# All 1024 base columns through seven block products of 512 columns, instead of 96 plain ones beside products of 464

## The reference, cut to what matters

```python
y = einsum('si,oi->so', x[b], cond_weight[id[b]])        # stage one: adapter of this element
base = einsum('td,od->to', y, base_W) + base_b            # stage two: 1024 x 1024 base product
logits = einsum('td,nd->tn', y, router_W) + router_b      # 15 router columns
probs = softmax(logits); top-8 of 15, summed per expert   # 8 gates per token
h = einsum('td,erd->ter', y, A)                           # 8 experts of rank 16 = 128 columns
out[b] = x[b] + base + einsum('ter,eor->to', h * gate, B) * 2
```

## Time and profile before

| | |
|---|---|
| median of three runs | 402.02 us |
| the profiled execution, device time | 402.37 us |
| its span, first to last instruction | 400.5 us |
| TensorE matmuls busy | 394.4 us (98%), 2102 |
| VectorE busy | 301.1 us (75%), 553 |
| ScalarE busy | 158.5 us (40%), 225 |
| granted TensorE clock, mean | 1.000 of 2.4 GHz |
| one element, in the steady part | 48.10 us |

### The profile page before, as it was taken

The page is one execution under the profiler, slowest core; times in us unless marked ns, Lnnn a source line. Parts: engine busy times, 40 slices in busy tenths (PEclk is TensorE's granted clock), DMA queues, the critical chain, the costliest instruction groups (busy, mean ns, idle before and its releaser), DMA issues.

```text
span 400.5 us, 5982 instructions
## 1 busy us (share of the span) xinstructions
PE 394.4 (98%) x2102; PEld 348.0 (87%) x2102; DVE 301.1 (75%) x553; ACT 158.5 (40%) x225; POOL 8.1 (2%) x22
## 2 busy tenths in 40 slices
PE   7999999999999999999999999999999999999996
PEld 7788888888888988889888888888888888888985
DVE  2867998799868884789658886489856799467763
ACT  4656443573146401554026620355304542144300
POOL 0002220000000000000000000000000000000000
PEclk9999999999999999999999999999999999999999
DMA  7999498830467306663076510775026830464002
GB/s 286 401 391 395 88 200 270 308 110 0 157 210 263 105 0 209 187 232 105 0 255 220 195 63 14 261 276 182 0 86 228 304 115 0 149 219 158 2 0 105
DMA packets 27133, 67.56 MB, mean 169 GB/s; under 512 B 3442, under 2 KB 14194, under 8 KB 26994
## 3 DMA queue, kind: packets, MB, share of 16 engines
q1 hardware_dynamic: 25106, 62.47, 44.2%
q0 software_dynamic: 1872, 3.90, 4.9%
q10 hardware_dynamic: 144, 1.05, 0.7%
HBM read 58.08 MB, written 8.39 MB: 166 GB/s over the span
## 4 chain that ended last, share of the span: by engine, by line
PE 97%; DMA 1%; issue 0%; SPq 0%; DVE 0%
PE y_ps L807 29%; PE y_ps L809 15%; PE pl_ps L832 7%; PE x_ps L843 6%; PE x_ps L842 6%; PE x_ps L844 6%; PE s_ps L843 6%; PE s_ps L844 6%; PE s_ps L842 6%; PE pl_ps L833 4%; PE s_ps L857 1%; PE s_ps L859 1%; PE s_ps L858 1%; DMA w_raw<-in_wT 1%; PE y_ps L820 1%; PE x_ps L859 0%
## 5 line engine op out<-in xcount | busy, mean ns | idle before, releaser
L807 PE MATMUL y_ps<-x_split,w_hi 128*128 128x512 f32 x504 | 176.0, 393 | 0.9 <-issue 0.9
L809 PE MATMUL y_ps<-x_split,w_lo 128*128 128x256 f32 x504 | 141.2, 280 | 0.0
L807 PEld LDWEIGHTS y_ps<-x_split,w_hi 128*128 128x128 f32 x504 | 94.4, 187 | 22.7 <-issue 1.4
L809 PEld LDWEIGHTS y_ps<-x_split,w_lo 128*128 128x128 f32 x504 | 95.2, 189 | 0.3
L389 ACT CAST w_hi<-w_raw 128x1024 fp32r<-128x1024 f32 x59 | 61.8, 1050 | 75.5 <-DMA w_raw<-in_wT 75.5
L511 DVE TENSOR_TENSOR w_lo<-w_raw,w_hi 128x1024 fp32r<-128x1024 f32 x59 | 72.1, 1224 | 16.8 <-ACT w_hi L389 15.1
L381 ACT COPY y_sum<-y_ps 128x256 f32<-128x256 f32 x63 | 23.4, 372 | 62.2 <-PE y_ps L809 62.1
L832 PE MATMUL pl_ps<-pl_split,y_hi 128*128 128x480 f32 x128 | 42.7, 383 | 0.0
L529 DVE TENSOR_TENSOR y_sum<-y_ps,y_sum 128x256 f32<-128x256 f32 x63 | 26.5, 420 | 19.4 <-ACT y_sum L381 19.4
L833 PE MATMUL pl_ps<-pl_split,y_lo 128*128 128x240 f32 x128 | 34.9, 273 | 0.0
L842 PE MATMUL s_ps<-st_hi,y_hi 128*128 128x464 f32 x80 | 30.4, 380 | 0.0
(11 more groups left out here) (112 smaller groups left out, 537.8 us busy)
## 6 DMA issues: line engine op xcount, KB each, us to landing
w_raw<-in_wT SPq DMA_DIRECT2D x60, 512.0 KB, 3.4
res<-in_x SPq DMA_DIRECT2D x16, 512.0 KB, 4.5
x_raw<-in_xT SPq DMA_DIRECT2D x14, 512.0 KB, 4.8
out<-res SPq DMA_DIRECT2D x13, 512.0 KB, 3.0
early_raw<-in_wT SPq DMA_DIRECT2D x4, 512.0 KB, 8.6
hi_raw<-in_base_t SPq DMA_DIRECT2D x2, 928.0 KB, 10.3
st_raw<-in_base_t SPq DMA_DIRECT2D x2, 928.0 KB, 11.9
st_raw<-in_base_t POOLq DMA_DIRECT2D x2, 928.0 KB, 9.7
```

Source lines behind the costliest of these rows:

```text
L807: nc.tensor.matmul(y_ps[:, c % 2, :], w_hi[:, s, k, :], x_split[:, k, :, :].rearrange("p s t -> p (s t)"), start=(k == 0), stop=False)
L809: mm = nc.tensor.matmul(y_ps[:, c % 2, 0:T], w_lo[:, s, k, :], x_split[:, k, 0, :], start=False, stop=(k == KC - 1))
```

## The change

The 96 plain base columns are gone. `pl_split` holds only the 144 adapter and router columns, so the first matmuls of stage two are 288 and 144 columns wide instead of 480 and 240. The blocks of the base matrix are 512 columns wide instead of 464, and so is each matmul of the block products, each DMA that loads or adds a block, and each cast and subtraction on a block. The two loads of plain columns, their two casts and two subtractions in element 0, and the two additions of plain columns into `res` in each element go. What TensorE waits for before the first matmuls of an element's stage two is now the sum `ar_sum` of the element before, not the second of these additions.

The wider blocks need room in SBUF: the transposed gate operand and two arrays used with it now lie in the second half of weight slot 3 of `w_hi`, and three small arrays share space. The number and order of TensorE's instructions are the same.

```diff
-    NP = 96
-    NH = (D - NP) // 2
-    PL = AR + NP
     DH = D // 2
-    N1, PLAIN, N2 = slice(0, NH), slice(NH, NH + NP), slice(NH + NP, D)
...
-        pl_split = sb("pl_split", [P, KC, 2, PL], F32R)
+        pl_split = sb("pl_split", [P, KC, 2, AR], F32R)
...
-        st_raw, st_hi, st_lo = split_pair("st", [P, KH, 7, NH])
+        st_raw, st_hi, st_lo = split_pair("st", [P, KH, 7, DH])
...
-        at_hwt = spot[0]
-        hwt_hi = sb("hwt_hi", [P, NT, P], F32R)
-        hwt_lo = sb("hwt_lo", [P, NT, P], F32R)
+        at_hwt = at_w + (W_SLOTS - 1) * 4 * KC * P + 4 * KH * P
+        hwt_hi = sb("hwt_hi", [P, NT, P], F32R, over=at_hwt)
+        hwt_lo = sb("hwt_lo", [P, NT, P], F32R, over=at_hwt + 4 * NT * P)
...
-            for h in range(2):
-                load_plain(h)
-            load_block(hi_raw[:, :, T4, :], 0, N1, r00_in)
+            load_block(hi_raw[:, :, T4, :], 0, H1, r00_in)
...
-                if c in (5, 6):
-                    plain_hi(c - 5)
...
-                add_plain(b)
-                dve.wait_ge(pl_added, b + 1)
...
-                        nc.tensor.matmul(pl_ps[:, t, 0:2 * PL], hi, pl_split[:, k, :, :].rearrange("p s n -> p (s n)"), start=(k == 0), stop=False)
-                        mm = nc.tensor.matmul(pl_ps[:, t, 0:PL], lo, pl_split[:, k, 0, :], start=False, stop=(k == KC - 1))
+                        nc.tensor.matmul(pl_ps[:, t, 0:2 * AR], hi, pl_split[:, k, :, :].rearrange("p s n -> p (s n)"), start=(k == 0), stop=False)
+                        mm = nc.tensor.matmul(pl_ps[:, t, 0:AR], lo, pl_split[:, k, 0, :], start=False, stop=(k == KC - 1))
...
-                dst = ps[:, at]
+                dst = ps[:, :]
...
-                pe.wait_ge(pl_added, b)
+                pe.wait_ge(ar_sum_done, b)
                 plain(b)
...
-            add_block(st_raw[:, :, T2, :], base_t[:, KH:KC, N2], t2_in)
+            add_block(st_raw[:, :, T2, :], base_t[:, KH:KC, H2], t2_in)
```

More of the change, by code:

```diff
@@ L140, in adaln_ffn_kernel @@
         shift = sb("shift", [P, NT, NR])
-        picked = sb("picked", [P, NT, NR], over=at_shift)
         row_max = sb("row_max", [P, NT])
-        prob = sb("prob", [P, NT, NR])
+        prob = sb("prob", [P, NT, NR], over=at_shift)
+        picked = sb("picked", [P, NT, NR], over=at_maps)
         row_sum = sb("row_sum", [P, NT])
@@ L149, in adaln_ffn_kernel @@
         gate_n = sb("gate_n", [P, NT, E])
+        at_ar = spot[0]
         ar_sum = sb("ar_sum", [P, NT, AR])
+        router_raw = sb("router_raw", [P, KC, NR], over=at_ar)
         def bank(name, shape):
@@ L168, in adaln_ffn_kernel @@
         ar_in = sem("ar_in")
-        pl_in = [sem(f"pl_in{h}") for h in range(2)]
         r00_in = sem("r00_in")
@@ L404, in ar_part @@
                 act.wait_ge(ar_done, 2 * b + 2)
-                nc.scalar.copy(ar_sum[:, :, :], pl_ps[:, :, PL:PL + AR]).then_inc(ar_part_done, 1)
+                nc.scalar.copy(ar_sum[:, :, :], pl_ps[:, :, AR:AR + AR]).then_inc(ar_part_done, 1)
             def make_x_hi(b):
@@ L647, in stage2 @@
                 dve.wait_ge(x_ps_done, x_adds(b, 2))
-                take(0, N2, x_ps[:, AT1]).then_inc(x_added, 1)
+                take(0, H2, x_ps[:, :]).then_inc(x_added, 1)
                 make_hwt_lo(b)
@@ L656, in stage2 @@
                 dve.wait_ge(z_added, z_adds(b, 1))
-                take(1, N2, x_ps[:, AT1]).then_inc(x_added, 1)
+                take(1, H2, x_ps[:, :]).then_inc(x_added, 1)
                 if second:
@@ L764, in _ @@
             dve.wait_ge(p1_done, 1)
-            take(0, N2, w_ps[:, AT1]).then_inc(p1_added, 1)
+            take(0, H2, w_ps[:, :]).then_inc(p1_added, 1)
             routing_logits(0)
@@ L768, in _ @@
             dve.wait_ge(p1_done, 2)
-            take(1, N2, x_ps[:, AT1]).then_inc(p1_added, 1)
+            take(1, H2, x_ps[:, :]).then_inc(p1_added, 1)
             t1_lo()
@@ L821, in stage1_float32, with plain @@
                 mm.then_inc(y_ps_done, 1)
-            def plain(b, first=False):
+            def plain(b):
                 for t, part in ((1, 0), (0, 0), (1, 1), (0, 1)):
                     for k in PLAIN_ORDER[:KC - 2] if part == 0 else PLAIN_ORDER[KC - 2:]:
-                        if first and t == 1 and k in (0, KH):
-                            pe.wait_ge(pl_lo_done, k // KH + 1)
                         if t == 1 and k < KH:
@@ L869, in first_stage2 @@
                 pe.wait_ge(ar_lo_done, 2)
-                plain(0, first=True)
+                plain(0)
                 pe.wait_ge(blocks_lo_done, 1)
@@ L879, in first_stage2 @@
                 pe.wait_ge(t_lo_done, 1)
-                product(z_ps, y_block(0, 0), T1, at=AT2)
+                product(z_ps, y_block(0, 0), T1)
                 pe.wait_ge(hw_done, 1)
@@ L883, in first_stage2 @@
                 pe.wait_ge(blocks_lo_done, 3)
-                product(z_ps, y_block(1, 0), B11, begins=False, at=AT2)
+                product(z_ps, y_block(1, 0), B11, begins=False)
                 pe.wait_ge(b_lo_done, 1)
@@ L889, in first_stage2 @@
                 lora_b(1, x_ps, H1).then_inc(x_ps_done, 1)
-                product(v_ps, y_block(0, 1), T1, at=AT2)
-                product(v_ps, y_block(1, 1), B11, begins=False, at=AT2)
+                product(v_ps, y_block(0, 1), T1)
+                product(v_ps, y_block(1, 1), B11, begins=False)
                 lora_b(1, v_ps, H2).then_inc(v_ps_done, 1)
             def stage2(b):
-                pe.wait_ge(pl_added, b)
+                pe.wait_ge(ar_sum_done, b)
                 plain(b)
@@ L900, in stage2 @@
                 pe.wait_ge(z_added, z_adds(b, 0))
-                product(z_ps, s_block(S1), T1, at=AT2).then_inc(z_ps_done, 1)
+                product(z_ps, s_block(S1), T1).then_inc(z_ps_done, 1)
                 pe.wait_ge(t_lo_done, 2)
@@ L914, in stage2 @@
                 pe.wait_ge(s4_lo_done, b)
-                product(z_ps, y_block(0, 1), B11, begins=False, at=AT2)
+                product(z_ps, y_block(0, 1), B11, begins=False)
                 pe.wait_ge(hwt_lo_done, b + 1)
```

66 lines of the change are left out of this document (19 added, 47 removed).

## The result

The kernel after took 407.53 us (median of four runs, 407.22 to 408.11), the kernel before 402.10 us on the same chip (four runs, 401.26 to 402.84): a ratio of 1.0128, 95% interval 1.0103 to 1.0153. The prediction said 407.5. The profiled execution after took 407.73 us with a span of 405.9 us, against 402.37 and 400.5. The size is right, and partly by luck: one of the terms that should make it up is missing, and one nearly three times as large that was not forecast stands in its place.

What follows compares the result with a forecast made beforehand. TensorE, busy 98% of the span, was taken as the bound. Element 0 +1.28, element 1 +1.83 and elements 2 to 7 +2.35 gave +5.5 us on the 402.02 us median: 407.5 us, range 404.0 to 409.3.

Steps and rivals of the forecast that it cites:

- Products dearer: Block products, 464 to 512 columns: each matmul 0.0189 us longer, +1.59 us an element, +1.81 in element 0.
- First matmuls: Stage two's 16 pairs, narrowed to 288 and 144 columns: 0.2455 us a pair instead of 0.3300, about -1.35 us an element.
- The floor: Behind stage two's narrow matmul: the next weights' load keeps the following matmul at least 0.11 us away, despite only 144 columns.
- First product of element 0: Start of element 0's products: TensorE waits for the first `st_lo`, until 36.35 instead of 35.52, +0.83 us.
- `y_lo` in element 1: After 12 first pairs of element 1's stage two, TensorE waits 1.26 us for `y_lo` pair 3.
- T4 late: Element 1's stage one: the adding DMA's block T4 lands near 66.2 instead of 63.9, delaying chunk 3 by 0.4 us.
- `y_lo` in elements 2 to 7: After 12 first pairs of stage two, TensorE waits for `y_lo` pair 3, 0 to 0.32 us each, 0.91 us together.
- no floor: Rival on stage two's narrow matmul: pair costs 0.206 us, but waits grow; +4.1, 406.1 us; chance 10%.
- columns decide: Rival: weight loads hide behind 144 columns and `y_lo` is there in time; -2.9, 399.1 us; chance 5%.
- The waits don't bind: Rival: the floor holds, but VectorE, rid of some work, is early enough; +2.1, 404.1 us; chance 14%.
- element 0's `hwt_lo`: VectorE stays some 0.4 us ahead there; the margins-overrun rival had it up to 0.7 us late, 409.0 us, chance 9%.

Runs made afterwards that it cites:

- the run with 240 columns: The kernel after with the narrow first matmul of stage two 240 instead of 144 columns wide, the extra columns' result unused; 407.04 us.
- the run with small matmuls: The kernel after with one added 16-column matmul at the start of stage one in elements 1 to 7, result overwritten; 406.93 us.

## Why the prediction was right in size, point by point

- **Products dearer, +1.59 us an element: right, a little too large.** 84 product matmuls took 17.73 us before (7.56 + 7.64 + 2.53 in element 2) and 19.24 after: 0.2111 and 0.2290 us, +1.51. I had priced the old width by the first 36, 0.2100; over all 84 it is 0.2111.
- **First matmuls -1.36 us: right.** -1.41; a pair is 0.242, not 0.2455 us. The floor is shown by the loads 0.11 us apart and by the run with 240 columns. Widths together are +0.06 us in elements 2 to 7 instead of +0.24.
- **First product of element 0, +0.83: right,** 0.78, with the subtraction 2.28 us long as forecast.
- **`y_lo` in element 1, +1.26: mechanism right, too large.** It is 0.73. `y_lo` came 3.57 us after the stretch began (84.34 to 87.91), not 4.05. The term that was mis-sized is the 3.87 us that it started from. It was read from one execution, and was a late one: the second execution of the kernel before has 3.40, and the two runs of it with small matmuls 3.44 and 3.45; only the one with the gate operand moved, whose element 0 began earlier, was later still, 4.47. From 3.40, the forecast's own steps (+0.18, +0.16, -2.95) give 0.79. That the wait of stage one gave VectorE time does not explain it: with 0.28 us of that wait instead of 1.02, in the run with 240 columns, `y_lo` came at 3.63.
- **T4 late, +0.4: mechanism right, place off, and another cause on top.** T4 landed at 65.1, not 66.2, so chunk 3 wasn't late (the first adding DMA was issued at 45.31, 0.16 us later than before and not 0.95). VectorE ended the sum of chunk 1 1.4 us later than before, and that is worth about 0.3 us before chunk 4: 0.28 and 0.30 in the runs with 240 columns and with small matmuls. The other 0.7 of the 1.02 us is the transfer of chunk 4's weights, which was not in the forecast. The total is inside the bounds of 0 to 1.2, but not by what they stood for. Why that transfer landed late stays open; it runs beside the adding DMAs, and no run here separates them.
- **`y_lo` in elements 2 to 7, +0.91: failed.** No wait came. The step that failed is "None of that moves with the change, since it hangs on the end of stage one". It holds only while stage one keeps its pace: the other engines' work behind it takes its own time, so a stage one that is 0.41 us longer lets `y_lo` come earlier against its end (2.74 us in element 2 instead of 2.89). At the quick pace the waits are there, some 1.1 us.
- **Not forecast at all: stage one slower by 0.41 us in six elements, +2.46 us.** The step that failed is that stage one stands in the sum with nothing, without a reason given; its instructions are the same, its price is not. Its rows held only element 1 (22.60), and a look at element 2 (22.19) would have shown two prices for the same work.

By cause, after minus before: widths +0.8 (forecast +2.1), waits +2.5 (forecast +3.4), slow pace +2.5 (forecast 0), earlier start of this execution -0.5 (forecast 0), and 0.1 more in stage one of elements 0 and 1. That 5.4 stands beside 5.5 is luck: errors that cancel, among them 0.7 us of late weights, which the run with 240 columns does not have, and a start of stage one that is 0.5 us earlier than before (it lies anywhere from 10.5 to 12.2 us in these runs). Without the slow pace the forecast's own terms give +3.3 here, and with the `y_lo` waits that come back some +4.4: the direction rested on the waits of elements 0 and 1, the floor and the widths, and that part holds. The run with the small matmul in elements 1 to 7 comes near that kernel: its span is 4.6 us above before, with 0.8 us of added matmuls in it.

Of the rivals, "no floor" and "columns decide" are refuted by the run with 240 columns. "The waits don't bind" is right for six elements, but not for the reason given: VectorE is not early by the work that it was rid of, as the run with small matmuls shows. Nothing ran over in element 0's `hwt_lo`.

## What to carry to other kernels

A trade of columns between matmuls is not a trade of columns. Here a matmul of 144 columns cost about what one of 240 did, the 0.11 us that the next weights take, so 96 plain columns were on the edge where the narrow matmul is paid in full, and taking them away saved only the wide one's part. Before an unchanged stage is put down as costing the same, compare its price in every element of the trace: where it has two, a shift of a tenth of a microsecond upstream can move it from one to the other, and that was here worth as much as all waits. A margin that is read from one execution is a sample: the 3.87 us of `y_lo` in element 1 was 3.40 in the next execution of the same kernel. When a stage in front of a wait gets slower, look whether the wait went away by it, and don't count both.

## What the runs showed of the hardware that was not expected

- **One stream of matmuls has two paces at the same clock.** Pairs of 512 and 256 columns: 0.3467 us (832 cycles of 2.4 GHz) or 0.3533 us (848), granted clock 1.00 in both. One 16-column matmul ahead flips it, either way; so did waits between chunks; element 0 had either pace from the same instructions; and once it flipped at a chunk where TensorE had not waited. All this fits a pace that hangs on the moment at which the stream goes on, but no run sets that moment by itself. Contention with other traffic is possible, but the DMA shares of the two paces overlap (in elements 1 to 7 0.50 to 0.78 slow, 0.53 to 0.79 quick; in element 0 1.05 at either), so the rate of transfers alone doesn't decide. What fixes the pace is open.
- **A recorded start of a matmul can come before its columns,** as I read the row at 134.12 (0.34 us instead of 0.30, behind a matmul shorter than the load of weights); the next load's start is the better mark.
- **Added work can take no time or four times its own.** The same seven 16-column matmuls, 0.8 us, changed the time from the start of element 1 to the end of the span by -1.3 us in the kernel after (345.3 to 344.0) and by +2.9 us in the kernel before (340.5 to 343.4).
